# Loading and making in one program what the next one needs first: a chain of six on-chip programs

## The chip, the cores and the metric

One Trainium2 chip, one of its cores. The metric is the device time of one launch in microseconds. A core has five engines with instruction queues of their own: TensorE (PE: matrix products and transposes into PSUM banks), VectorE (DVE), ScalarE (ACT), GpSimd (POOL) and SyncE (SP), which issues the DMAs here. They are ordered against each other by semaphores alone.

## What is computed

A transformer-like chain over x of shape (16, 256, 128), with a context of (16, 64, 128). Every step is `x = x + f(layernorm(x))`:

```python
x = x + _L0_xattn_ref(_layernorm(x), ctx, mask, Wq, Wkv, Wout, b_out)      # cross attention, 16 heads
x = x + _L0_ffn_ref(_layernorm(x), Wqkv, q_scale, k_scale, Wo, ...)        # 6 layers: local attention + gated FFN
x = x + _L1_xattn_ref(_layernorm(x), ctx, ctx, projection)                 # kernel (random feature) attention
x = x + _L1_ffn_ref(_layernorm(x), clip_x, clip_down, w_gate, w_up, w_down) # FFN with rounded weights
x = x + _L2_xattn_ref(_layernorm(x), ctx, Wk1, ..., gamma, beta)           # causal + context attention, 3 norms
x = x + _L2_ffn_ref(_layernorm(x), W_fc, ln_w, ln_b, W_proj)               # FFN with ternary weights
x = x + _L3_xattn_ref(_layernorm(x), ctx, W, b)                            # context attention
x = x + _L3_ffn_ref(_layernorm(x), Ws, bs, W1, b1, W2, b2)                 # 8 experts, top-k of the tokens each
```

In the six layers q and k are normed per head, scaled by q_scale and k_scale, and rotated by fixed tables (cosine, sine, a position's scale). The ternary weights are `sign(W) * min(round(|W| / (mean(|W|) + 1e-6)), 1)`, a mean over the whole matrix.

## The kernel before

x stays in SBUF as x_all (128 partitions, 32 tiles of 128 tokens by 128 features). The work goes over it in 8 passes of 512 tokens (4 tiles); several stages split the passes into two groups of Q = 4. Six programs run one after the other, each in a block of its own: every engine gets a list of instructions in an order written out by hand, with waits on semaphores (`wait_ge`) between engines. At the end of a block all engines meet, SyncE clears the program's semaphores one by one (`clear`), and the next block begins. Names of tiles carry the program's letter:

- **x_**, `cross_attention`. The key and query weights, and the value and output weights, are multiplied together first (`fold`); then for each of 64 half tiles TensorE makes scores, VectorE lowers and weighs them, ScalarE takes exponentials, TensorE mixes. VectorE writes the normed sum into s_all.
- **f_**, `shifted_layers`. 6 layers times 8 passes, run as a hardware loop of 48 passes. At its start it loads the rotation tables' constants (L664 to L667), the first layer's weights and the first layer's Wv and Wo; TensorE folds these pair by pair (L805), ScalarE copies them (L1494) into w_vo; VectorE multiplies six layers' tables (rot_all, L1134), SyncE writes them to DRAM (rot_dram, L680) and reads the first layer's back (L636). VectorE clears k_t, vo_off and x_shifted among others (L1121 to L1129). Every engine then adds to the counters that the loop expects. In the loop SyncE issues the shifts of values and x, and the next layer's weights.
- **k_**, `kernel_attention_and_ffn`. Loads the context twice (ctx_t, and ctx_1 with a column of ones), the projection and the weights; x_all plus s_all is formed by VectorE and GpSimd; phi_k comes from ctx_t and proj, its products with ctx_1 (`values`, L1827) need it and GpSimd's constants. ScalarE copies them, then norms x (L2059).
- **a_**, `two_attentions`. Norms, causal attention, context attention and a two-layer FFN in phases, group by group. `take_stats` and `roots` on VectorE (12 short instructions a root), norms on ScalarE (L2648), `scale_and_shift` of each norm (two products or sums of 128x512) on GpSimd (L2481, L2483), `last_sum` on VectorE (L2572).
- **g_**, `ternary_ffn`. Loads W_fc and W_proj, measures the mean (VectorE, then a partition_all_reduce on GpSimd), makes ternary weights, takes the statistics of x; then per pass: turn, up, gelu, norm of h, down, add.
- **y_, e_**, `experts`. Loads for the context attention, then the experts' weights; statistics of x, attention, routing, then selection and the experts.

The order at the start of ternary_ffn on VectorE, as an example of how such a queue is written:

```python
            measure()
            roots(0)
            make_ternary()
            roots(1)
            for i in range(1, PASSES + 4):
                if i <= PASSES:
                    roots_of_h(i - 1)
                if 3 <= i <= PASSES + 2:
                    add(i - 3)
```

## Time and profile before

| | |
|---|---|
| three runs | 4461.14, 4453.69, 4463.28 us; median 4461.14 |
| profiled execution | 4456.33 us, its span 4454.5 us |
| PE busy | 3964.2 us (89%) |
| DVE busy | 3584.2 us (80%) |
| ACT busy | 2960.2 us (66%) |
| POOL busy | 2206.9 us (50%) |
| mean granted clock of TensorE | 0.931 |
| DMA | 251.24 MB, mean 56 GB/s |

The span runs from the first to the last instruction. Busy shares are averages over six programs with different limits. The granted clock is a share of TensorE's full speed; 0.5 would be the lower of its two levels all the time. In the rows further down, `PEld` is TensorE's weight load, `SPq` a DMA issued on SyncE's queue, `L830` a line of the kernel; `f_bank<-f_w_qk,f_xs_t` is output and inputs; `x2` the instructions in the row; in brackets stands the idle time of that engine just before, and what ended it.

### The profile page before, as it was taken

The numbers are of one execution on the slowest core, as the hardware profiler recorded it, in microseconds if no ns is written. First come the engines' busy times: TensorE is split into PE (matmuls) and PEld (weight loads), VectorE is DVE, ScalarE is ACT, GpSimd is POOL, SyncE is SP. The second block draws the span as 40 slices with busy tenths as digits, with TensorE's granted clock in tenths as the row PEclk, the third lists the DMA queues.
The fourth block names the chain that finished last, engine by engine and source line by source line (L and its number), as shares of the span: only waits on it lengthen the run. The fifth ranks groups of instructions, "written<-read, shape, count | busy, mean of one in ns | idle before, by whom it ended". The sixth has DMA issues, their size and how long they took to land. (4 is left out here: it accounts for less than half of the span.)

```text
span 4454.5 us, 117888 instructions
## 1 busy us (share of the span) xinstructions
PE 3964.2 (89%) x43247; PEld 2386.8 (54%) x43247; DVE 3584.2 (80%) x8496; ACT 2960.2 (66%) x5496; POOL 2206.9 (50%) x1392
## 2 busy tenths in 40 slices
PE   8978999999999999999999999999999855737735
PEld 5644555555555555555555555555555533525534
DVE  6887999899998999989999899989999655356341
ACT  3425787787777777777787787777778545636402
POOL 0005666666666666666666666666666400130006
PEclk9989999999999999999999999999999966868658
DMA  1012232333233332233232332232323200000102
GB/s 43 1 40 65 66 68 64 83 68 69 65 69 82 69 70 65 65 84 70 65 68 64 83 73 64 64 85 65 70 64 68 50 15 12 1 5 18 72 7 37
DMA packets 188120, 251.24 MB, mean 56 GB/s; under 512 B 88676, under 2 KB 129382, under 8 KB 187366
## 3 DMA queue, kind: packets, MB, share of 16 engines
q1 hardware_dynamic: 182054, 240.47, 23.2%
q0 software_dynamic: 5632, 4.33, 0.7%
q8 instruction: 352, 5.77, 0.6%
q14 instruction: 82, 0.67, 0.0%
HBM read 41.65 MB, written 14.30 MB: 13 GB/s over the span
## 5 line engine op out<-in xcount | busy, mean ns | idle before, releaser
L1419 POOL TENSOR_TENSOR f_rot_a<-f_rot_a,f_rot_b 128x1024 f32<-128x1024 f32 x384 | 908.1, 2370 | 311.8 <-DVE f_rot_b L1160 206.6
L1427 POOL TENSOR_TENSOR f_rot_a<-f_rot_a,f_norm 128x1024 f32<-128x1024 f32 x384 | 731.3, 1905 | 648.5 <-DVE f_norm L1178 525.4
L844 PE MATMUL f_bank<-f_w_vo,f_xs_t 128*32 128x512 f32 x6144 | 815.8, 603 | 0.2
L1157 DVE TENSOR_TENSOR f_rot_a<-f_bank,f_rot 128x512 f32<-128x512 f32 x768 | 523.0, 682 | 76.2 <-ACT f_squares L1519 40.4
L1528 ACT ACTIVATE f_vo<-f_bank 128x512 f32<-128x512 f32 x768 | 458.6, 597 | 170.2 <-PE f_bank L844 162.6
L1519 ACT ACTIVATE f_squares<-f_bank 128x512 f32<-128x512 f32 x768 | 455.8, 594 | 113.1 <-PE f_bank L830 67.1
L1540 ACT ACTIVATE f_k_t<-f_bank 64x512 f32<-64x512 f32 x768 | 452.7, 589 | 102.7 <-PE f_bank L866 98.2
L1160 DVE TENSOR_TENSOR f_rot_b<-f_bank,f_rot 128x512 f32<-128x512 f32 x768 | 505.9, 674 | 0.0
L1433 POOL TENSOR_TENSOR f_prob<-f_score,f_stat 128x512 f32<-128x512 f32 x384 | 400.6, 1043 | 192.1 <-DVE f_stat L1210 187.7
L1164 DVE TENSOR_REDUCE f_sums<-f_squares 128x16 f32<-128x1024 f32 x384 | 464.5, 1210 | 4.7 <-ACT f_squares L1519 4.7
L876 PEld LDWEIGHTS f_bank<-f_k_t,f_q_t 128*32 128x32 f32 x12288 | 345.4, 110 | 179.4 <-issue 99.5
L900 PEld LDWEIGHTS f_bank<-f_vo_off,f_prob_t 128*32 128x32 f32 x6144 | 330.8, 110 | 167.3 <-issue 150.7
L830 PE MATMUL f_bank<-f_w_qk,f_xs_t 128*128 128x512 f32 x768 | 400.5, 603 | 22.2 <-DMA f_w_qk<-in_Wqk 7.9
L876 PE MATMUL f_bank<-f_k_t,f_q_t 128*32 128x128 f32 x12288 | 406.0, 273 | 1.2 <-ACT f_bank L1546 0.6
L900 PE MATMUL f_bank<-f_vo_off,f_prob_t 128*32 128x128 f32 x6144 | 406.8, 274 | 0.2
L900 PE MATMUL f_bank<-f_vo,f_prob_t 128*32 128x128 f32 x6144 | 406.8, 274 | 0.0
L836 PE MATMUL f_bank<-f_w_qk,f_xs_t 128*128 128x512 f32 x768 | 401.7, 605 | 0.7 <-DVE f_rot_b L1160 0.7
L1533 ACT ACTIVATE f_q_t<-f_bank 128x512 f32<-128x512 f32 x384 | 227.9, 594 | 260.2 <-PE f_bank L860 260.2
L900 PEld LDWEIGHTS f_bank<-f_vo,f_prob_t 128*32 128x32 f32 x6144 | 330.8, 110 | 0.0
L1206 DVE TENSOR_REDUCE f_stat<-f_score 128x8 f32<-128x512 f32 x384 | 259.9, 677 | 76.8 <-ACT f_score L1550 71.9
L866 PEld LDWEIGHTS f_bank<-ident,f_rot_a 128*128 128x128 f32 x1536 | 180.4, 141 | 217.7 <-issue 153.8
L1198 DVE TENSOR_REDUCE f_stat<-f_bank 128x8 f32<-128x512 f32 x384 | 257.7, 671 | 29.1 <-PE f_bank L876 23.6
(446 smaller groups left out, 7372.8 us busy)
## 6 DMA issues: line engine op xcount, KB each, us to landing
f_vo_off<-f_vo SPq DMA_DIRECT2D x1152, 128.0 KB, 2.3
f_vo_off<-f_vo SPq DMA_DIRECT2D x384, 64.0 KB, 2.0
f_w_qk<-in_Wqk SPq DMA_DIRECT2D x12, 512.0 KB, 5.3
f_vo_dram<-f_vo_pair SPq DMA_DIRECT2D x48, 128.0 KB, 1.8
f_x_shifted<-s_all SPq DMA_DIRECT2D x48, 128.0 KB
f_x_shifted<-s_all SPq DMA_DIRECT2D x48, 127.0 KB
f_w_vo<-f_vo_dram SPq DMA_DIRECT2D x10, 512.0 KB, 5.4
e_w<-in_e_W SPq DMA_DIRECT2D x2, 2048.0 KB, 12.7
```

What stands on the lines that cost most here:

```text
L836: nc.tensor.matmul(flat(Q), chunk_x(t), w_qk[:, 0, 512 * g:512 * g + 512], start=True, stop=True).then_inc(q_done, 1)
L844: done = nc.tensor.matmul(bank[V][32 * w:32 * w + 32, :], x[:, at:at + 32], w_vo[:, 4 * g:4 * g + 4, w // 2, :], start=True, stop=True)
L876: done = nc.tensor.matmul(bank[S][32 * w:32 * w + 32, 128 * b:128 * b + 128], q_t[:, g, 128 * b + 32 * w:128 * b + 32 * w + 32], k_t[:, :, ...
L900: done = nc.tensor.matmul(bank[Y][32 * w:32 * w + 32, 0:128], prob_t[:, g, 128 * b + 32 * w:128 * b + 32 * w + 32], source[:, g, 2 * (t % ...
L1157: nc.vector.tensor_tensor(rot_a[:, slot, n, :].rearrange("p (h d) -> p h d", h=GROUP), source, c_tab, ALU.mult)
L1160: nc.vector.tensor_tensor(rot_b[:, g, n, :].rearrange("p (h s d) -> p h s d", h=GROUP, s=2), swapped, s_tab, ALU.mult).then_inc((q_rotated ...
L1164: nc.vector.tensor_reduce(sums[:, g, :], squares[:, g, :, :].rearrange("p n (h d) -> p (n h) d", h=GROUP), AX_X, ALU.add).then_inc(lengths, 1)
L1419: nc.gpsimd.tensor_tensor(rot_a[:, slot, :, :], rot_a[:, slot, :, :], rot_b[:, g, :, :], ALU.add).then_inc(rot_summed, 1)
L1427: nc.gpsimd.tensor_tensor(heads, heads, over(norm[:, 16 * g:16 * g + 16], [128, 16, HEAD_DIM]), ALU.mult).then_inc(qk_normed, 1)
L1519: nc.scalar.activation(squares[:, g, n, :], flat((Q, K)[n]), ACT.Square).then_inc((q_squared, k_squared)[n], 1)
L1528: nc.scalar.activation(vo[:, g, 2 * (t % 2) + j, :], flat(V), ACT.Copy).then_inc((va_copied, vb_copied)[j], 1)
L1540: done = nc.scalar.activation(k_t[r:r + 64, n, 4 * g:4 * g + 4, at:at + 128], flat(T)[r:r + 64, :].rearrange("p (b n) -> p b n", b=4), ACT ...
```

## The change

What a program needs first is loaded or made in the one ahead, in tiles that outlive it; the context (ctx_t, ctx_1) is held from the first program to the last.

- `cross_attention` gets, behind its x loads: the tables' constants, the first layer's Wv, Wo and other weights, ctx_1; GpSimd makes the mask `band` and the six tables one by one, SyncE writes them and reads the first back; TensorE folds the first layer's Wv and Wo behind its last mixing, ScalarE copies them.
- `shifted_layers` loses all of that. Its ScalarE shifts the first x before it adds to its counters. The clears of k_t, vo_off and x_shifted go from VectorE to GpSimd. SyncE issues four loads for kernel_attention_and_ffn ahead of the last layer.
- `kernel_attention_and_ffn` loses its loads and the waits for them.
- `two_attentions` loses the load of ctx_t, takes the first pass's root ahead of the others, loads the ternary program's weights and makes them ternary (in the tile h, which is not yet used), takes the next program's statistics, and in its second group gives the last scale and shift of every second pass to VectorE.
- `ternary_ffn` loses its loads, statistics and ternary weights; it loads for `experts` and takes the statistics and the first half of the roots for it.
- `experts` loses its six small loads, the statistics and the first roots.

The diff, cut to its core:

```diff
+            sp.wait_ge(fold_made, 4)
+            sp.dma_start(rot_const, dram["rot"]).then_inc(const_in, 16)
+            sp.dma_start(head_scale, dram["qk_scale"]).then_inc(const_in, 16)
+            sp.dma_start(band_in[:, :, :], dram["band"]).then_inc(const_in, 16)
+            sp.wait_ge(fold_made, 8)
+            sp.dma_start(w_v[:, :, :], dram["Wv_t"][0:PAIRS].rearrange("b p n -> p b n")).then_inc(next_in, 16)
+            for n in range(2):
+                half = slice(64 * n, 64 * n + 64)
+                sp.dma_start(w_out[half, :, n, :], dram["Wo"][0:PAIRS].rearrange("b p n -> p b n")[half]).then_inc(next_in, 16)
...
+            sp.dma_start(kept["w_qk"][:, :, :], first_of("Wqk").rearrange("a p n d -> (a p) n d")).then_inc(kept_in, 16)
...
+            for layer in range(DEPTH):
+                sp.wait_ge(rot_made, layer + 1)
+                sp.dma_start(rot_dram[layer], rot_part[layer % 2]).then_inc(rot_out[layer % 2], 16)
+            sp.wait_ge(rot_out[0], 16 * (DEPTH // 2))
+            sp.wait_ge(rot_out[1], 16 * (DEPTH // 2))
+            sp.dma_start(kept["rot"][:, :, :, :].rearrange("p a n d -> p (a n d)"), rot_dram[0]).then_inc(kept_in, 16)
+            sp.wait_ge(kept_in, 112)
...
+            pool.wait_ge(zeroed, 4)
+            pool.wait_ge(const_in, 48)
+            nc.gpsimd.tensor_copy(kept["band"][:, :, :], band_in[:, :, :]).then_inc(band_made, 1)
+            pool.wait_ge(band_made, 1)
+            for layer in range(DEPTH):
+                if layer > 0:
+                    pool.wait_ge(rot_made, layer)
+                if layer >= 2:
+                    pool.wait_ge(rot_out[layer % 2], 16 * (layer // 2))
+                nc.gpsimd.tensor_tensor(rot_part[layer % 2].rearrange("p (a n d) -> p a n d", a=2, n=4), rot_const,
+                                        head_scale[:, layer].unsqueeze(1).broadcast_to([128, 2, 4, 64]), ALU.mult).then_inc(rot_made, 1)
...
+            def fold_next(b):
+                if b == 0:
+                    pe.wait_ge(next_in, 48)
+                if b < 2:
+                    pe.wait_ge(unit_made, 8 * PASSES)
+                else:
+                    pe.wait_ge(lowered, N - 3 + b)
+                to = (unit_bank + score_bank)[b]
+                for k in range(2):
+                    last = nc.tensor.matmul(to[:, 256 * k:256 * k + 256], w_v[:, 2 * b + k, :], w_out[:, 2 * b + k, :, :], start=True, stop=True)
+                last.then_inc(next_folded, 1)
...
+            for b in range(4):
+                fold_next(b)
...
+                act.wait_ge(next_folded, b + 1)
+                nc.scalar.activation(w_vo_next[:, 2 * b:2 * b + 2, :, :].rearrange("p b n d -> p (b n d)"), (unit_bank + score_bank)[b][:, :], ACT.Copy).then_inc(next_made, 1)
...
             sp.wait_ge(zeroed, 2)
             load_pair(0)
-            sp.wait_ge(rot_made, DEPTH)
-            sp.dma_start(rot_dram.rearrange("l p n -> p l n"), rot_all.rearrange("p l a n d -> p l (a n d)")).then_inc(rot_out, 16)
-            sp.wait_ge(rot_out, 16)
-            load_rot(0, 0)
-            load_rot(1, 0)
-            for semaphore in (w_qk_in[0], w_qk_in[1], ln_in, w_2_in, rot_in[0], rot_in[1]):
-                good_for_layer(semaphore, 0)
-            good_for_layer(w_1_in, 0, 32)
+            for semaphore in (w_qk_in[0], w_qk_in[1], w_vo_in[0], w_vo_in[1], ln_in, w_2_in, rot_in[0], rot_in[1]):
+                sp.sem_inc(semaphore, PASSES * 16)
+            sp.sem_inc(w_1_in, PASSES * 32)
+            sp.wait_ge(off_zeroed, 2)
...
+            for name, to in following["loads"]:
+                sp.dma_start(to, dram[name]).then_inc(following_in, 16)
...
-            nc.vector.memset(wo_first, 0.0).then_inc(zeroed, 1)
-            chain.mark(nc.vector.memset(xs_t[:, :, :], 0.0))
+            nc.vector.memset(xs_t[:, :, :], 0.0).then_inc(zeroed, 1)
+            nc.vector.memset(wo_pair[:, :, :], 0.0).then_inc(zeroed, 1)
             chain.mark(nc.vector.memset(gate[:, :, :], 0.0))
-            chain.mark(nc.vector.memset(wo_pair[:, :, :], 0.0))
-            chain.mark(nc.vector.memset(k_t[:, :, :, :], 0.0))
-            chain.mark(nc.vector.memset(vo_off[:, :, :, :], 0.0))
-            chain.mark(nc.vector.memset(x_shifted[:, :, :], 0.0))
             chain.wait()
             chain.mark(nc.vector.memset(gate[ONES_ROW:ONES_ROW + 1, 2, :], 1.0))
-            dve.wait_ge(const_in, 48)
-            chain.link(nc.vector.tensor_copy(band[:, :, :], band_in))
-            nc.vector.nop().then_inc(zeroed, 1)
-            for layer in range(DEPTH):
-                nc.vector.tensor_tensor(rot_all[:, layer], rot_const, head_scale[:, layer].unsqueeze(1).broadcast_to([128, 2, 4, HEAD_DIM]), ALU.mult).then_inc(rot_made, 1)
-            dve.wait_ge(rot_made, DEPTH)
...
+            pool.wait_ge(x_taken[0], 1)
+            nc.gpsimd.memset(k_t[:, :, :, :], 0.0).then_inc(k_t_cleared, 1)
+            pool.wait_ge(k_t_cleared, 1)
+            nc.gpsimd.memset(vo_off[:, :, :, :], 0.0).then_inc(off_zeroed, 1)
+            pool.wait_ge(off_zeroed, 1)
+            nc.gpsimd.memset(x_shifted[:, :, :], 0.0).then_inc(off_zeroed, 1)
+            pool.wait_ge(off_zeroed, 2)
...
-            for b in range(4):
-                act.wait_ge(first_folded, b + 1)
-                nc.scalar.activation(w_vo[:, 2 * b:2 * b + 2, :, :].rearrange("p b n d -> p (b n d)"), flat(b), ACT.Copy).then_inc(w_vo_in[b // 2], PASSES * 8)
             act.wait_ge(zeroed, 2)
             act.wait_ge(s_opened, 1)
-            act.wait_ge(rot_out, 16)
+            def shift_in(s, p):
+                act.wait_ge(x_turned[s], p + 1)
+                source = bank[F][:, 0:SEQ]
+                nc.scalar.activation(xs_t[0:64, s, :], source[0:64, :], ACT.Copy).then_inc(xs_made[s], 1)
+                nc.scalar.activation(xs_t[64:128, s, 1:SEQ], source[64:128, 0:SEQ - 1], ACT.Copy).then_inc(xs_made[s], 1)
+            shift_in(0, 0)
...
+            sp.dma_start(next_w[:, 0, :], dram["g_fc"]).then_inc(next_in, 16)
+            sp.dma_start(next_w[:, 1, :], dram["g_proj"]).then_inc(next_in, 16)
+            sp.dma_start(following["affine"][:, :, :], dram["g_affine"]).then_inc(next_in, 16)
...
-                for i in range(Q):
+                for i in range(0, Q, 1 if g == 0 else 2):
...
+            def next_stats(p, count):
+                dve.wait_ge(summed, count)
+                at = PASS_TILES * (p % Q)
+                for t in range(PASS_TILES):
+                    chain.mark(nc.vector.bn_stats(stats[:, 0, at + t, :], tile(of_pass(x_all, p), t)))
+                chain.wait()
+                for t in range(PASS_TILES):
+                    chain.mark(nc.vector.bn_aggr(following["mv"][:, PASS_TILES * p + t, :], stats[:, 0, at + t, :]))
+            def measure():
+                dve.wait_ge(next_in, 48)
+                nc.vector.tensor_reduce(size[:, :, 0], next_w, AX_X, ALU.add, apply_absolute_value=True).then_inc(sized, 1)
+            def make_ternary():
+                dve.wait_ge(size_sum, 1)
+                chain.link(nc.vector.tensor_scalar(size[:, :, 2], size[:, :, 1], 1.0 / (DIM * PASS_TOK), 1e-6, ALU.mult, ALU.add))
+                chain.link(nc.vector.reciprocal(size[:, :, 3], size[:, :, 2]))
+                for k in range(2):
+                    chain.mark(nc.vector.tensor_scalar(w_tern[:, k, :], next_w[:, k, :], size[:, k, 3:4], 0.5, ALU.mult, ALU.is_gt))
+                chain.wait()
+                for k in range(2):
+                    chain.mark(nc.vector.tensor_scalar(next_w[:, k, :], next_w[:, k, :], size[:, k, 3:4], -0.5, ALU.mult, ALU.is_lt))
+                chain.wait()
+                nc.vector.tensor_tensor(w_tern[:, :, :], w_tern[:, :, :], next_w, ALU.subtract).then_inc(tern_made, 1)
+            def scale_and_shift(p):
+                dve.wait_ge(hatted[3], p + 1)
+                tiles = [128, PASS_TILES, 128]
+                source, to = (ap.rearrange("p (t n) -> p t n", n=128) for ap in (hat[:, p % Q, :], n[:, p % Q, :]))
+                chain.wait()
+                dve.wait_ge(y3_made, p + 1)
+                chain.link(nc.vector.tensor_tensor(to, source, rows[:, GAMMA, :].unsqueeze(1).broadcast_to(tiles), ALU.mult))
+                chain.link(nc.vector.tensor_tensor(to, to, rows[:, BETA, :].unsqueeze(1).broadcast_to(tiles), ALU.add))
...
             def phase_0(g):
                 for i in range(Q):
                     take_stats(0, Q * g + i, of_pass(x_all, Q * g + i))
-                roots(0, g, 1e-5)
+                    if g == 0 and i == 0:
+                        roots(0, g, 1e-5, slice(0, PASS_TILES))
+                roots(0, g, 1e-5, slice(0 if g else PASS_TILES, GROUP_TILES))
...
             def phase_6(g):
-                for i in range(Q):
-                    last_sum(Q * g + i)
+                if g == 0:
+                    for i in range(Q):
+                        last_sum(i)
+                    for i in range(Q):
+                        next_stats(i, Q)
+                else:
+                    for p in range(Q, PASSES, 2):
+                        scale_and_shift(p + 1)
+                        last_sum(p + 1)
+                        next_stats(p + 1, p + 1)
+                        last_sum(p)
+                        next_stats(p, p + 2)
             phase_0(0)
-            dve.wait_ge(first_in, 112)
+            dve.wait_ge(first_in, 96)
             nc.vector.tensor_copy(causal[:, :], causal_in[:, :]).then_inc(causal_made, 1)
             phase_0(1)
+            measure()
             dve.wait_ge(rest_in, 80)
             nc.vector.tensor_tensor(beta_b2[:, :], rows[:, BETA, :], rows[:, B2, :], ALU.add).then_inc(beta_made, 1)
             for i in STEPS:
                 phase_2(0, i)
+            make_ternary()
...
-            measure()
             roots(0)
-            make_ternary()
             roots(1)
             for i in range(1, PASSES + 4):
                 if i <= PASSES:
                     roots_of_h(i - 1)
                 if 3 <= i <= PASSES + 2:
                     add(i - 3)
+                    next_stats(i - 3)
+                    if i - 3 == Q:
+                        next_roots()
         @block.scalar
...
-            for g in range(GROUPS):
-                for p in range(Q * g, Q * g + Q):
-                    take_stats(Y, p)
-                roots(Y, g)
+            roots(Y, 1)
...
+                    by, on = shift[:, k, at:at + 1], var[:, k, 1, at:at + 1]
+                    if k == Y and p < Q:
+                        by, on = given["shift"][:, at:at + 1], given["var"][:, 1, at:at + 1]
...
```

## Rows read from the trace of the kernel before

**Rows 1.** Windows by stage: us, busy us per engine, granted clock, DMA share, GB/s.
```profile
344.70:3586.80 3242.10, 3189.05 (x39070) 1844.09 (x39068) 2916.44 (x6208) 2471.75 (x4508) 2048.03 (x1247) 0.99 0.30 68
```

**Rows 2.** Timeline, end of the first program, start of the layers program.
```profile
304.96 2.05 PE L296 MATMUL x_bank<-x_vo,x_prob_t 128*128 128x128 f32 x16
...
310.09 1.12 DVE L375 TENSOR_SCALAR s_all<-x_all,x_s_mv,x_s_var 128x128 f32<-128x128 f32 x4
313.65 0.33 SPq L664 DMA_DIRECT2D f_q_t<-in_rot  x1
...
319.25 3.90 DVE L1125 MEMSET f_k_t<- 128x4608 f32 x1 [0.91 <-issue]
...
339.45 0.81 SPq L636 DMA_DIRECT2D f_rot<-f_rot_dram  x2
...
341.91 2.04 PE L830 MATMUL f_bank<-f_w_qk,f_xs_t 128*128 128x512 f32 x2 [7.46 <-ACT f_xs_t L1510]
...
348.31 2.36 POOL L1419 TENSOR_TENSOR f_rot_a<-f_rot_a,f_rot_b 128x1024 f32<-128x1024 f32 x1 [13.85 <-DVE f_rot_b L1160]
```

**Rows 3.** Timeline, first 60 us: a fold on TensorE, a GpSimd memset.
```profile
10.05 0.94 POOL L204 MEMSET x_w_q<- 64x1024 f32 x1
...
27.96 3.62 PE L235 MATMUL x_bank<-x_w_out,x_w_v 128*128 128x256 f32 x16
```

**Rows 4.** Timeline, start of the kernel-attention program.
```profile
3598.44 0.20 POOL L1813 MEMSET k_ones<- 128x128 f32 x1
...
3604.46 7.06 PE L1827 MATMUL k_bank<-k_ctx,k_phi_k 64*32 64x129 f32 x32 [0.77 <-ACT k_phi_k L2140]
```

**Rows 5.** Timeline, start of the two-attentions program.
```profile
3758.49 6.26 ACT L2648 ACTIVATE a_xn<-x_all,a_shift,a_var 128x128 f32<-128x128 f32 x16 [13.24 <-DVE a_shift L2514]
```

**Rows 6.** Timeline of VectorE, middle of the two-attentions program.
```profile
3826.01 0.42 DVE L2536 TENSOR_REDUCE a_top<-a_bank 128x4 f32<-128x256 f32 x1 [9.71 <-PE a_bank L2354]
```

**Rows 7.** Timeline of VectorE, its second half begins.
```profile
3916.46 0.68 DVE L2528 TENSOR_TENSOR a_y<-a_att,a_xn 128x512 f32<-128x512 f32 x1
...
3922.17 0.39 DVE L2536 TENSOR_REDUCE a_top<-a_bank 128x4 f32<-128x256 f32 x1
```

**Rows 8.** Timeline of all engines, end of the two-attentions program.
```profile
3986.56 1.26 POOL L2481 TENSOR_TENSOR a_n<-a_hat,a_rows 128x512 f32<-128x512 f32 x1
3986.63 1.74 DVE L2572 SCALAR_TENSOR_TENSOR x_all<-a_n,x_all 128x512 f32<-128x512 f32 x1 [4.48 <-POOL a_n L2483]
...
3995.30 0.69 DVE L2572 SCALAR_TENSOR_TENSOR x_all<-a_n,x_all 128x512 f32<-128x512 f32 x1 [1.15 <-POOL a_n L2483]
```

**Rows 9.** Timeline, start of the ternary program.
```profile
3999.33 0.33 SPq L2860 DMA_DIRECT2D g_w<-in_g_fc  x1
...
4004.12 0.86 DVE L2923 BATCH_NORM_STATS2 g_stats<-x_all 128x6 f32<-128x128 f32 x4
...
4008.95 0.17 DVE L2934 TENSOR_SCALAR g_var<-g_mv 128x16 f32<-128x16 f32 x1
...
4011.52 3.19 ACT L2994 ACTIVATE g_xn<-x_all,g_shift,g_var 128x128 f32<-128x128 f32 x8 [22.99 <-DVE g_shift L2936]
...
4013.57 1.23 DVE L2949 TENSOR_TENSOR g_w_tern<-g_w_tern,g_w_cmp 128x1024 f32<-128x1024 f32 x1
...
4016.00 0.60 ACT L3001 ACTIVATE g_xn_t<-g_bank 128x512 f32<-128x512 f32 x1 [1.29 <-PE g_bank L2875]
```

**Rows 10.** Timeline of VectorE, end of ternary, start of the last.
```profile
4090.24 2.47 DVE L2955 BATCH_NORM_STATS2 g_h_stats<-g_h 128x6 f32<-128x512 f32 x4 [2.87 <-ACT g_h L3008]
...
4109.35 0.69 DVE L2974 TENSOR_TENSOR x_all<-x_all,g_bank 128x512 f32<-128x512 f32 x1 [6.71 <-PE g_bank L2890]
```

**Rows 11.** Timeline of ScalarE, start of the last program.
```profile
4120.76 1.65 ACT L3303 ACTIVATE y_xn<-x_all,y_shift,y_var 128x128 f32<-128x128 f32 x4 [15.34 <-DMA y_ctx_rows<-in_ctx_rows]
```

**Rows 12.** Timeline of SyncE, start of the last program.
```profile
4111.52 0.33 SPq L3127 DMA_DIRECT2D y_w<-in_y_W  x1
```

**Rows 13.** One line of VectorE in the layers program.
```profile
L1171 DVE TENSOR_SCALAR f_norm_y<-f_norm_y x194: 170/181/2324, 353.7 to 3557.2; 128x32 int32<-128x32 int32 x146, 128x36 int32<-128x36 int32 x46, 128x4 int32<-128x4 int32 x2
```

255 lines of the change are left out of this document (111 added, 144 removed).

## The prediction

> **What bounds the kernel now.** I read the windows by stage first. The layers program takes 3242 us with TensorE busy for 3189 of them at a granted clock of 0.99 [rows 1]; the loads and first steps of every program lie outside that stretch, so its steady loop gets nothing from this change and no edit is aimed at it. What is left is the seams between the six programs, and there I read the timeline of all engines. At the first seam VectorE ends the first program at 311.2, SyncE issues the first load of the next at 313.65, but TensorE starts projecting only at 341.91, because ScalarE waits for a round trip of the rotation tables through DRAM, whose last leg is issued at 339.45 [rows 2]. In the other seams the reader is to see who holds the first norm or product: in kernel-attention the product of phi_k and the context's values, at 3604.46 [rows 4]; in the ternary program VectorE's statistics and roots, ScalarE's norm following at 4011.52 and its copy of the turned tile at 4016.00 [rows 9]; in the last program a DMA, to 4120.76 [rows 11].
>
> **The change part by part, and its sum.** Times are of the profiled execution.
>
> *First program's end.* Behind the last mixing product (ends 307.0 [rows 2]) TensorE gets four folds of two products each, the 16 matmuls that take 3.62 us in [rows 3]; ScalarE's last copy then ends near 307.0 + 3.6 + 0.8 = 311.4 to 311.5, against VectorE's 311.2 [rows 2]: +0.3. At the lower clock the folds could take twice that: bound +3.9. The loads for it (SyncE issues twelve for constants, weights and context, six writes of tables and one read back) come after the x loads; nothing stands behind them on SyncE but the end of the program, 260 us later. GpSimd's cast and six products lie in the first 60 us or so; each can hold a VectorE operation of two SBUF inputs as the 1.74 against 0.69 in [rows 8] shows, 1.05 us for at most seven: 0 to +7, and I take +0.5, since most of VectorE's work there reads PSUM or one input. Semaphores are cleared one by one: 3.34 us lie between VectorE's end at 3995.99 [rows 8] and the next program's 3999.33 [rows 9], 52 semaphores, and 1.48 between 4110.04 [rows 10] and 4111.52 [rows 12], 18 semaphores: 0.055 each. Nine more here: +0.5.
>
> *Start of the layers.* Gone are the wait for first_in, eight folds, six table products and the round trip. What still stands before the first projection, from SyncE's 313.65: VectorE starts 0.5 later and clears xs_t, wo_pair and gate (0.48, 0.27, 1.34, 0.17 of gap, 0.48 by size, at the 0.85 ns an element of the 3.90 us clear [rows 2]), then adds to its counters; SyncE's three loads and counters and ScalarE's two copies end sooner. So TensorE begins near 313.65 + 3.7 = 317.4 instead of 341.91: -24.5. GpSimd now clears k_t, vo_off and x_shifted, 9216 elements a partition at 0.94 us for 1024 [rows 3], 8.5 us behind its 0.4 us copy: free near 323.2. Its first sum was at 348.31 [rows 2], so it is due at 323.8: covered by 0.6 us. Were that cover gone and the clears to count in full: +8. What waits for them on other queues (ScalarE's first k copy, SyncE's first shift) comes later still.
>
> *In the layers.* Four loads for kernel-attention are issued on SyncE ahead of the last layer, some 0.4 us each; behind them stand the shifts of values. SyncE waits for ScalarE there, so 0, with +1.7 as the bound.
>
> *Kernel-attention.* Its products of phi_k no longer wait for the context's load. Next to be late is GpSimd's last constant, done at 3598.64, against 3604.46 [rows 4]: -5.7. ScalarE's chain of copies, norms and rounding follows on it; the roots it needs next do not depend on a load and were done before the products began to matter.
>
> *Two attentions, start.* The roots are split, one pass first. VectorE's second root chain costs another 2.45 us (that of 16 tiles, 4008.95 to 4011.4 [rows 9]), so the norms of passes 1 to 3 start at 3758.5 + 2.45 = 3760.9. Three passes of 6.26 / 4 us [rows 5] end at 3765.6, against 3764.7: ScalarE's copy of the turned tile stands behind all four norms, so the early start of one buys nothing: +0.9.
>
> *Two attentions, middle.* The ternary weights take about 3.5 us of VectorE (4011.3 to 4014.8, [rows 9]), behind the second phase; VectorE has 9.7 us of idle time before 3826.01 [rows 6]: 0. The statistics of the first four passes (4004.12 to 4008.95, 4.8 us, [rows 9]) stand ahead of VectorE's additions from 3916.46, and it goes from these without a gap into the scores at 3922.17, for which ScalarE and TensorE wait [rows 7]: +4.8, in full.
>
> *Two attentions, end.* GpSimd's four passes of two 1.26 us products become two, VectorE takes the other two and all statistics: the roots end at 3982.15 (3986.63 less the 4.48 of idle time), ScalarE's second norm 3.1 us later, and from there on, 3985.4, it has four products (0.69), four sums (0.69) and four times 1.2, 10.3 us, ending at 3995.7, as before [rows 8] if nothing collides. But a VectorE operation with two SBUF inputs, begun under a GpSimd product, ended 0.55 us behind it (1.74 instead of 0.69, [rows 8]). Followed through, three such meetings add 1.0 us each: ends 0 to +5, taken +3.0. This is what the Trainium skill, SBUF — State Buffer, section Who interferes with whom, says: the two engines exclude each other for the whole instruction when VectorE has two SBUF inputs. It speaks against giving VectorE this work; by it the term is +3, without it 0.
>
> *Ternary program.* Only the roots stay before the first norm: 3999.4 + 2.5 = 4001.9, two norms of 3.19 us to 4005.1, then the copy that came at 4016.00 [rows 9]: -10.9. Statistics for the next program (1.2 a pass) fit the idle time before the next statistics of h, 2.87 us at the shortest [rows 10]; where next_roots (2.45) is added they do not: 1.2 + 2.45 - 2.87 = +0.8. The last pass has no cover, +1.2.
>
> *Last program.* ScalarE's first norm at 4111.6 instead of 4120.76 [rows 11, 12]: -9.1; the expert weights' loads move ahead and are needed much later. Five semaphores fewer over the later programs: -0.3.
>
> Sum: 0.3 + 0.5 + 0.5 - 24.5 - 5.7 + 0.9 + 4.8 + 3.0 - 10.9 + 0.8 + 1.2 - 9.1 - 0.3 = -38.5. The profiled execution took 4456.3 (4454.5 of span and 1.8 around it): 4417.8. It lies 4.8 below the median of three runs, 4461.1; from that, 4422.6. I take 4420.
>
> **Rivals.**
> 1. GpSimd becomes the bound at the start of the layers: its clears cost more than 9 us and the counters that wait for them hold the first shift. For it: the cover is only 0.6 us. Against it: the price is read from like clears. +8: 4428.
> 2. The change does less than it says: a program's first instructions come late for reasons other than its data. In the layers' start TensorE waited for ScalarE, but ScalarE's own 6 us were for nothing the trace names, and some of it may be its long row of counters, which still stands there. A third of -24.5 lost, and part of the others: +12, 4432.
> 3. Slower. The layers' 48 passes of 67.5 us [rows 1] are entered with GpSimd and VectorE at another phase to each other. VectorE's L1171 usually takes 0.18 us but once 2.32, under a GpSimd sum [rows 13]; if the loop locks into such meetings, +0.8 us a pass undoes all, and +0.9 gives 4420 + 43 = 4463. Against it: the loop is TensorE's, busy for 98% of it, and its order is unchanged.
> 4. No change within the measurement: the same at +0.8 a pass.
>
> **How the numbers follow.** Forecast 0.70, rival 1 0.12, rival 2 0.10, rival 3 0.05, rival 4 0.03. Below the forecast lie the case without collisions (-3), and the runs' own spread (4453.7 to 4463.3); so 4404 at the low end. Upward the bounds of the folds, of GpSimd's work in the first program and rivals 1 and 2: 4440. About 0.2% (9 us) is what a measurement of this kernel can tell from no change: faster 0.92, same 0.03, slower 0.05.
>
> **What would show it.** The layers' first projection some 4 us after the program's first instruction; in kernel-attention the phi_k products right behind GpSimd's last constant; in two attentions the four norms ending about 1 us later, 4.8 us of statistics ahead of the second half's additions, the last sums of x_all at VectorE and not GpSimd; the ternary program's first copy under 7 us from its start; the last program's first norm at once. The layers' stretch of about 3242 us must stand. It is wrong if that moves by over 10 us, if the first seam keeps more than 10 us, or if GpSimd's or VectorE's operations grow in the first program.

## The result, and the profile after

The changed kernel takes 4416.48 us (median of four runs, 4414.45 to 4419.71) where the kernel before took 4461.64 (four runs, 4453.69 to 4463.28): 45.2 us less, a ratio of 0.990 with a 95% interval from 0.9888 to 0.9912. The profiled execution took 4414.45, its span 4412.6, against 4456.33 and 4454.5: 41.9 less. Two further sets of runs of the changed kernel gave 4415.14 and 4415.52, against 4463.02 and 4461.80 of the kernel before beside them. The 4463.02 is the median of the seven fast runs of that control, without two slow ones of 5139.95 and 12955.43 us.

To see where the time went I read the same event in both timelines, one seam after the other, and note how much earlier it comes in the kernel after. All rows until the experiments are of the profiled execution of the kernel after, in its timeline, unless said otherwise.

**Something nobody edited comes first.** Before (first fence), GpSimd stands idle for 7.67 us ahead of the select that makes the identity matrix, and every engine's first program waits for that; after (second fence), it stands idle for 0.51 us. The first load is issued at 2.60 instead of 9.77: 7.17 us, and the prediction has no word of it.

```profile
8.76 0.28 POOL L3697 TENSOR_SCALAR_AFFINE_SELECT ident<-ident 128x128 f32<-128x128 f32 x1 [7.67 <-issue]
```

```profile
1.59 0.29 POOL L3746 TENSOR_SCALAR_AFFINE_SELECT ident<-ident 128x128 f32<-128x128 f32 x1 [0.51 <-POOL ident_bf L3743]
...
2.60 0.39 SPq L195 DMA_DIRECT2D x_w_k<-in_x_Wk  x1
```

**The first seam** (answers to [rows 2] and [rows 3]). The folds are there, 3.62 us, and the last copy of them ends at 305.62, under VectorE's last operation, 305.72: they cost nothing. VectorE's first operation of the layers comes at 309.46, TensorE projects at 312.14, where it was at 341.91. GpSimd's clears end at 318.10; behind them it copies x once more, until 318.66, which the prediction's account leaves out, and its first sum follows on that without idle time, at 318.63. The rotation that the sum needs is done at 318.45. So nothing is left of the cover of 0.6 us that the prediction gave the clears.

```profile
299.47 2.05 PE L345 MATMUL x_bank<-x_vo,x_prob_t 128*128 128x128 f32 x16
...
301.36 3.62 PE L358 MATMUL x_bank<-x_w_out,x_w_v 128*128 128x256 f32 x16
...
304.61 1.11 DVE L439 TENSOR_SCALAR s_all<-x_all,x_s_mv,x_s_var 128x128 f32<-128x128 f32 x4
305.02 0.60 ACT L536 ACTIVATE f_w_vo<-x_bank 128x512 f32<-128x512 f32 x1 [0.27 <-PE x_bank L358]
...
309.46 0.48 DVE L1151 MEMSET f_xs_t<- 128x512 f32 x1 [3.74 <-PEq L66]
...
310.01 3.94 POOL L1434 MEMSET f_k_t<- 128x4608 f32 x1
...
312.14 2.04 PE L860 MATMUL f_bank<-f_w_qk,f_xs_t 128*128 128x512 f32 x2 [1.45 <-DVEq L1157]
...
317.17 1.28 DVE L1180 TENSOR_TENSOR f_rot_b<-f_bank,f_rot 128x512 f32<-128x512 f32 x2
...
318.27 0.39 POOL L1430 COPY f_xw<-s_all 128x256 f32<-128x256 f32 x1 [0.17 <-POOL f_x_shifted L1438]
...
318.63 2.35 POOL L1446 TENSOR_TENSOR f_rot_a<-f_rot_a,f_rot_b 128x1024 f32<-128x1024 f32 x1
```

In the first program itself one operation of VectorE shows GpSimd's new work, a product that takes 0.69 us elsewhere and began under a GpSimd product:

```profile
43.37 1.38 DVE L428 TENSOR_TENSOR x_prob<-x_score,x_stat 128x512 f32<-128x512 f32 x1
```

**The layers**, in the view by windows (answers to [rows 1]; from the first rotation to the last sum): 3242.07 us, TensorE busy for 3190.90, granted clock 0.99. The same two events lie 3241.34 apart before. The second row is a stretch of two attentions to which I come below.

```profile
314.96:3557.03 3242.07, 3190.90 (x39070) 1845.84 (x39068) 2916.83 (x6208) 2471.63 (x4508) 2051.65 (x1250) 0.99 0.30 68
3835.04:3866.43 31.39, 18.97 (x84) 13.21 (x83) 12.43 (x54) 14.77 (x34) 10.12 (x8) 0.73 0.00 1
```

**Kernel-attention** (answers to [rows 4]). The products of phi_k begin 0.05 us after GpSimd's last constant is done (3568.84 and 0.20). From the first row to the last, the first norm, 19.36 us pass; before it was 25.67 (3586.06 to 3611.73).

```profile
3557.03 0.69 DVE L1274 TENSOR_TENSOR s_all<-s_all,f_bank 128x512 f32<-128x512 f32 x1 [4.76 <-PE f_bank L981]
3561.98 0.10 POOL L1820 MEMSET k_plus<- 128x1 f32 x1 [56.33 <-POOLq L66]
...
3568.84 0.20 POOL L1825 MEMSET k_ones<- 128x128 f32 x1
...
3569.09 7.08 PE L1839 MATMUL k_bank<-ctx,k_phi_k 64*32 64x129 f32 x32 [3.48 <-POOL k_ones L1825]
...
3576.39 3.17 ACT L2069 ACTIVATE k_xn<-x_all,k_shift,k_var 128x128 f32<-128x128 f32 x8
```

**Two attentions.** At its start (answers to [rows 5]) the first norm is early, the other three wait for the second root chain, and the copy of the turned tile is at 3729.26, 14.33 us after VectorE's first statistics; before it was 13.51.

```profile
3718.63 1.65 ACT L2716 ACTIVATE a_xn<-x_all,a_shift,a_var 128x128 f32<-128x128 f32 x4 [9.62 <-DVE a_shift L2529]
...
3724.63 4.72 ACT L2716 ACTIVATE a_xn<-x_all,a_shift,a_var 128x128 f32<-128x128 f32 x12 [4.35 <-DVE a_shift L2529]
...
3729.26 0.57 ACT L2733 ACTIVATE a_xn_t<-a_bank 128x512 f32<-128x512 f32 x1
```

In the middle (answers to [rows 7]) 4.7 us of statistics (L2597) stand between the last sum of x_all and the additions, and the scores at 3893.21 come after them all:

```profile
3882.08 0.69 DVE L2590 SCALAR_TENSOR_TENSOR x_all<-a_n,x_all 128x512 f32<-128x512 f32 x1 [1.17 <-POOL a_n L2496]
3882.81 0.87 DVE L2597 BATCH_NORM_STATS2 a_stats<-x_all 128x6 f32<-128x128 f32 x4
...
3887.52 0.66 DVE L2543 TENSOR_TENSOR a_y<-a_att,a_xn 128x512 f32<-128x512 f32 x1
...
3893.21 0.39 DVE L2551 TENSOR_REDUCE a_top<-a_bank 128x4 f32<-128x256 f32 x1
```

At the end (answers to [rows 8]) VectorE's products and GpSimd's hold each other: VectorE's take 1.66 and 1.70 us where 0.69 is the usual price, and its next sum 1.63. The program ends 19.54 us after its last roots begin (3950.67 to 3970.21); before it was 16.31 (3979.68 to 3995.99).

```profile
3956.32 1.26 POOL L2496 TENSOR_TENSOR a_n<-a_n,a_rows 128x512 f32<-128x512 f32 x1
3956.48 1.66 DVE L2625 TENSOR_TENSOR a_n<-a_hat,a_rows 128x512 f32<-128x512 f32 x1 [3.33 <-ACT a_hat L2716]
3958.06 1.26 POOL L2494 TENSOR_TENSOR a_n<-a_hat,a_rows 128x512 f32<-128x512 f32 x1 [0.47 <-ACT a_hat L2716]
3958.17 1.70 DVE L2626 TENSOR_TENSOR a_n<-a_n,a_rows 128x512 f32<-128x512 f32 x1
...
3969.83 0.38 DVE L2600 BATCH_NORM_AGGREGATE g_mv<-a_stats 128x2 f32<-128x6 f32 x4
```

**Ternary and last program** (answer to [rows 9] and [rows 10 to 12]). Only roots stand ahead of the first norm; the copy comes 5.65 us after the program's first instruction at 3973.77, where it took 16.67. The last pass's statistics are uncovered, and then the last program norms at once.

```profile
3973.82 0.17 DVE L3003 TENSOR_SCALAR g_var<-g_mv 128x16 f32<-128x16 f32 x1 [3.61 <-PEq L66]
...
3976.33 3.18 ACT L3051 ACTIVATE g_xn<-x_all,g_shift,g_var 128x128 f32<-128x128 f32 x8 [16.81 <-DVE g_shift L3005]
...
3979.42 0.57 ACT L3058 ACTIVATE g_xn_t<-g_bank 128x512 f32<-128x512 f32 x1
```

```profile
4073.49 0.69 DVE L3030 TENSOR_TENSOR x_all<-x_all,g_bank 128x512 f32<-128x512 f32 x1 [5.39 <-PE g_bank L2952]
4074.22 0.87 DVE L2986 BATCH_NORM_STATS2 g_next_x_stats<-x_all 128x6 f32<-128x128 f32 x4
...
4076.85 1.65 ACT L3353 ACTIVATE y_xn<-x_all,yg_shift,yg_var 128x128 f32<-128x128 f32 x4 [7.28 <-PEq L66]
```

This table puts all traces of this study side by side, those of the experiments too. Each column is the distance between two events, in us: the start until the first load's issue; x from there to the last s_all operation of the first program; "to rot" from there to the layers' first rotation; the layers to their last sum; k to the last sum of kernel-attention; the gap to the first statistics of two attentions; a to the first norm of the ternary program; g to the first norm of the last one; y to the memset of ec_ones; and the rest of the span.

| trace | start | x | to rot | layers | k | gap | a | g | y | rest | span |
|---|---|---|---|---|---|---|---|---|---|---|---|
| before | 9.77 | 300.32 | 34.63 | 3241.34 | 161.47 | 3.62 | 260.37 | 109.24 | 130.90 | 202.84 | 4454.5 |
| before, again | 9.86 | 300.89 | 34.63 | 3241.54 | 161.82 | 3.62 | 261.23 | 107.76 | 131.70 | 205.55 | 4458.6 |
| before, no sum over partitions | 2.61 | 300.87 | 34.59 | 3247.66 | 162.03 | 3.63 | 261.33 | 107.36 | 133.86 | 203.66 | 4457.6 |
| first seam only | 9.80 | 303.58 | 10.28 | 3243.06 | 160.39 | 4.17 | 263.46 | 106.83 | 133.91 | 203.32 | 4438.8 |
| all but the first seam | 2.60 | 300.76 | 34.29 | 3244.52 | 154.77 | 3.52 | 264.32 | 100.59 | 132.26 | 203.87 | 4441.5 |
| after | 2.60 | 302.01 | 10.35 | 3242.07 | 154.25 | 3.65 | 261.40 | 100.52 | 132.35 | 203.40 | 4412.6 |
| after, again | 2.60 | 301.43 | 10.35 | 3241.88 | 154.26 | 3.65 | 261.41 | 100.52 | 132.37 | 203.23 | 4411.7 |
| after, third | 2.60 | 302.07 | 10.35 | 3244.15 | 154.82 | 3.64 | 259.73 | 99.35 | 132.17 | 205.42 | 4414.3 |
| clear of k_t twice | 2.60 | 302.88 | 10.35 | 3241.39 | 154.38 | 3.64 | 264.50 | 100.60 | 132.34 | 203.82 | 4416.5 |
| spare sum over partitions | 9.16 | 301.86 | 10.35 | 3244.14 | 154.14 | 3.65 | 259.77 | 99.36 | 133.76 | 204.51 | 4420.7 |
| statistics late | 2.61 | 300.89 | 10.35 | 3240.46 | 154.12 | 3.64 | 256.27 | 99.41 | 132.20 | 205.65 | 4405.6 |
| three pieces put otherwise | 2.60 | 301.99 | 10.35 | 3246.64 | 154.85 | 3.65 | 256.37 | 99.21 | 133.73 | 204.81 | 4414.2 |
| the same, again | 2.60 | 302.62 | 10.35 | 3238.03 | 154.80 | 3.64 | 256.36 | 99.20 | 133.69 | 204.21 | 4405.5 |

Between the rows "before" and "after" lie -7.2, +1.7, -24.3, +0.7, -7.2, 0.0, +1.0, -8.7, +1.4 and +0.6: -41.9 in all.

### The profile page after: what moved, and what is told of

Same layout as the page of the kernel before. It is cut to its first block and busy times, and to the rows that moved or that the text cites. A ratio compares the mean times of both kernels' runs of the same rounds, so it can differ in the third digit from the quotient of the medians.

```text
span 4412.6 us, 117906 instructions
## 1 busy us (share of the span) xinstructions
PE 3968.6 (90%) x43247; PEld 2389.2 (54%) x43247; DVE 3577.9 (81%) x8501; ACT 2960.0 (67%) x5496; POOL 2218.5 (50%) x1398
```

## The experiments

**The kernel before once more.** No edit; it is the control for the idle time at the start.

> The kernel before, once more, for its trace. The trace of before holds 7.67 us of idle time of GpSimd ahead of its first affine_select (line 3697), that of after 0.51 us there, though neither kernel was changed at that place. Theory A (it comes and goes between executions of any kernel): this trace may show either, and the other runs of this call a mixture. Theory B (it belongs to a program): about 7.7 us again here. Under B, 7.2 us of the 41.9 between the two profiled executions are not the seams' work but are still the changed program's; under A they are chance.

Measured: 4460.39 us (one run), and 7.76 us of idle time at that place. Against theory A, though one trace doesn't decide.

**The first seam alone.** The kernel before with the first program and the layers of the changed one; nothing is loaded in the layers for kernel-attention, and the context is loaded anew where it was.

```diff
-            cross_attention(nc, x_all, ident, arrays, s_all)
-            shifted_layers(nc, s_all, ident, ident_bf, arrays)
+            cross_attention(nc, x_all, ident, arrays, s_all, kept)
+            shifted_layers(nc, s_all, ident, ident_bf, arrays, kept, None)
```

> The kernel before with only the first part of the change: constants, rotation tables, folds and weights of the layers are made and loaded in the first program. Theory (each seam gives its own share): of the 41.9 us between the profiled executions 29.0 are there when the layers end, 7.2 of them at the very start; so 4461 - 22 = 4439 if the start is as in before, and 4432 if it is short, with the first projection under 4 us behind the layers' first instruction and the layers' stretch within 1.5 us of 3242. Rival (the layers lock into another phase against GpSimd): the stretch is over 10 us longer and the time over 4445.

Measured: 4442.60 us (five runs, 4436.50 to 4444.65) against 4459.98, ratio 0.9959 (0.9945 to 0.9972): 17.4 less. "To rot" is 10.28 as in the changed kernel, the layers' stretch 3243.06, the start long. So the seam gives what it should in its place and rival and theory part there in the theory's favour; but 5 us are lost elsewhere: x took 303.58, 2.9 more than the 300.7 on average of the four traces that have it unchanged, and two attentions, whose code is that of before, 263.46 instead of 260.4 to 261.3. The trace accounts for most of the 2.9: three of VectorE's products in the first program, 0.69 us alone, take 1.54, 1.28 and 1.75 under GpSimd's new operations, 2.5 us more.

**All but the first seam.** The changed kernel with the old first program (it loads the context's rows in addition) and the old start of the layers.

```diff
-                cross_attention(nc, x_all, ident, arrays, s_all, kept)
-                shifted_layers(nc, s_all, ident, ident_bf, arrays, kept, for_kq)
+            cross_attention(nc, x_all, ident, arrays, s_all, held)   # as before, and the rows of the context
+            shifted_layers(nc, s_all, ident, ident_bf, arrays, for_kq)   # as before, and the four loads ahead of the last layer
```

> The changed kernel with the first part undone: first program and start of the layers as before, all later seams as changed. Theory: the remaining 12.9 us of the trace, 4461 - 13 = 4448, and if the start is the short one 4441. Rival (the later seams give only part, some of it being clock): 4452 or more. With the first part alone the two gains should add up to the 45 us of the whole change within 5 us.

Measured: 4442.83 us (five runs, 4441.41 to 4444.06), ratio 0.9961 (0.9947 to 0.9974): 17.2 less, with the short start, where 4441 was expected; so the rival (4452 or more) falls. The two parts add up to 34.6, not to 45 within 5: additivity failed. The table says where. In the traces the two parts together are 28.7 and the whole 41.9; of the 13.2 between, 6.0 lie in two attentions (+3.1 and +4.0 in the parts, +1.0 in the whole), 4.2 in the layers (+1.7, +3.2, +0.7), 2.9 in y, 2.0 in x, less 2.3 in g, and the rest is small. None of that is at a seam: "to rot", k up to the first norm, and the ternary program's start are each what they are in the whole. This is a reading of one execution of each. But the medians of five runs are 10.6 us short as well, and the five of this kernel lie within 2.7 us, so the luck of one execution isn't enough to explain it. Why the parts give less than the whole isn't shown.

**Three pieces of two attentions put otherwise.**

```diff
 def phase_6(g):                       # g == 0
-                    for i in range(Q):
-                        next_stats(i, Q)
...
             roots(2, 1, EPS)
+            for i in range(Q):
+                next_stats(i, Q)
...
-                for i in range(0, Q, 1 if g == 0 else 2):      # GpSimd, last norm
+                for i in range(Q):
...
-                        scale_and_shift(p + 1)                 # VectorE, last phase
-                        last_sum(p + 1)
-                        next_stats(p + 1, p + 1)
                         last_sum(p)
-                        next_stats(p, p + 2)
+                        next_stats(p, p + 1)
...
-                    if g == 0 and i == 0:
-                        roots(0, g, 1e-5, slice(0, PASS_TILES))
-                roots(0, g, 1e-5, slice(0 if g else PASS_TILES, GROUP_TILES))
+                roots(0, g, 1e-5)
```

> The changed kernel with three of its pieces in two attentions put otherwise: the statistics of the first four passes stand behind the roots of the second norm of the second half (8.90 us of idle VectorE there) instead of ahead of its additions; the last norm's scale and shift is GpSimd's alone again, VectorE keeping the sums and statistics; and the first roots are one chain. Theory: -4.9 (statistics hidden), -1.9 (the end of the program 17.6 us behind the last roots instead of 19.5), -0.8 (the first copy): 7.6 us less than the changed kernel, about 4409. Rival 1: the idle time is not free, since ScalarE or TensorE run ahead of what they did and meet VectorE elsewhere: half of it, 4412. Rival 2: the statistics between the sums delay GpSimd's chain at the end by 1.2 us a pass: nothing won there, 4411.

Measured: 4405.97 us (four runs, 4404.34 to 4416.04), ratio 0.9878 (0.9862 to 0.9893), where 4409 was expected and the rivals had 4411 and 4412. Each piece can be read where it stands (the code numbers the norms of two attentions from 0 to 3, and so do I). The roots of norm 3 in the first half and of norm 1 in the second lie 32.14 us apart instead of 36.98: -4.84. The timeline of VectorE shows the statistics in their new place, done 4.2 us before anything is due:

```profile
3928.24 0.18 DVE L2529 SCALAR_TENSOR_TENSOR a_shift<-a_mv,a_var 128x16 f32<-128x16 f32 x1
3928.33 0.86 DVE L2594 BATCH_NORM_STATS2 a_stats<-x_all 128x6 f32<-128x128 f32 x4
...
3932.74 0.38 DVE L2597 BATCH_NORM_AGGREGATE g_mv<-a_stats 128x2 f32<-128x6 f32 x4
3937.30 0.69 DVE L2575 SCALAR_TENSOR_TENSOR a_h<-a_h 128x512 f32<-128x512 f32 x1 [4.19 <-ACT a_h L2803]
```

The end comes 17.69 us behind the last roots (3952.65 to 3970.34) instead of 19.54: -1.85. Here VectorE's statistics (0.87 for four, as without company) run under a GpSimd product undisturbed, while its sum, which reads two tiles, takes 1.65:

```profile
3960.87 1.59 POOL L2496 TENSOR_TENSOR a_n<-a_n,a_rows 128x512 f32<-128x512 f32 x1
3961.37 0.87 DVE L2594 BATCH_NORM_STATS2 a_stats<-x_all 128x6 f32<-128x128 f32 x4
...
3962.42 1.25 POOL L2494 TENSOR_TENSOR a_n<-a_hat,a_rows 128x512 f32<-128x512 f32 x1
3962.57 1.65 DVE L2587 SCALAR_TENSOR_TENSOR x_all<-a_n,x_all 128x512 f32<-128x512 f32 x1
...
3969.96 0.38 DVE L2597 BATCH_NORM_AGGREGATE g_mv<-a_stats 128x2 f32<-128x6 f32 x4
```

And the first copy comes 13.50 us after the first statistics instead of 14.33: -0.83. The sum of the three is 7.5, against 7.6 expected, so both rivals fall. The profiled execution was at the same time the slowest of the four (its layers took 3246.64).

**GpSimd's clear of k_t twice.**

```diff
+            nc.gpsimd.memset(k_t[:, :, :, :], 0.0).then_inc(off_zeroed, 1)
+            pool.wait_ge(off_zeroed, 1)
             nc.gpsimd.memset(k_t[:, :, :, :], 0.0).then_inc(k_t_cleared, 1)
...   # the later waits for off_zeroed go up by one
```

> The changed kernel with GpSimd's clear of k_t, 3.94 us, done twice at the start of the layers. In the changed kernel GpSimd was free at 318.66 and its first sum began at 318.63, so the cover is gone already. Theory (GpSimd's clears are now on the path there): the first sum comes 13.3 us behind the layers' first instruction instead of 9.3, and the end of the first pass, 217.3 us behind it, comes 3 to 4 us later. Rival (the wait is taken up by TensorE's row of passes, since the first sum feeds only a later product): the first sum is late and the first pass ends less than 1 us later.

Measured: 4418.30 us (one run). GpSimd's clears and its first two sums:

```profile
310.88 3.94 POOL L1434 MEMSET f_k_t<- 128x4608 f32 x1
...
314.88 3.94 POOL L1436 MEMSET f_k_t<- 128x4608 f32 x1
...
318.88 3.51 POOL L1438 MEMSET f_vo_off<- 128x4096 f32 x1
...
323.49 4.66 POOL L1448 TENSOR_TENSOR f_rot_a<-f_rot_a,f_rot_b 128x1024 f32<-128x1024 f32 x2
```

The first sum is 13.3 us behind TensorE's first instruction (310.20), as the theory says, and yet the first pass ends 216.99 us behind it (527.19), against 217.33 in the changed kernel (309.33 to 526.66). The theory falls and the rival stands: 4 us of delay on GpSimd at the start of the layers cost nothing. GpSimd's own idle stretches take them up. In the changed kernel it waits 2.61 us for VectorE ahead of its second sum and 7.77 us ahead of a later product:

```profile
323.60 2.34 POOL L1446 TENSOR_TENSOR f_rot_a<-f_rot_a,f_rot_b 128x1024 f32<-128x1024 f32 x1 [2.61 <-DVE f_rot_b L1180]
...
343.66 1.90 POOL L1454 TENSOR_TENSOR f_rot_a<-f_rot_a,f_norm 128x1024 f32<-128x1024 f32 x1 [7.77 <-DVE f_norm L1198]
```

With the second clear the two sums run back to back (x2 above), so the second is late by 1.3 us only, counted from TensorE's first instruction, and the product at the second place comes 0.4 us early, behind 6.11 us of idle time.

**The sum over partitions: left out before, doubled after.** Two kernels.

```diff
 # the kernel before, ternary program
-            nc.gpsimd.partition_all_reduce(size[:, :, 1], size[:, :, 0], 128, ...).then_inc(size_sum, 1)
+            nc.gpsimd.tensor_copy(size[:, :, 1], size[:, :, 0]).then_inc(size_sum, 1)
 # the changed kernel, ternary program
+            nc.gpsimd.memset(spare[:, :, 0], 1.0).then_inc(spare_set, 1)
+            pool.wait_ge(spare_set, 1)
+            nc.gpsimd.partition_all_reduce(spare[:, :, 1], spare[:, :, 0], 128, ...).then_inc(spare_set, 1)
```

> The kernel before, in which the ternary program's sum over partitions on GpSimd is left out (a plain copy stands in its place, so the weights' mean size is a partition's own). The idle time ahead of the first affine_select was 7.67, 7.76 and 7.71 us in the three traces in which that sum stands in the ternary program, and 0.51, 0.51 and 0.50 in the three in which it stands in two attentions, two programs of other loads. Theory A (the sum over partitions, by its place, makes GpSimd wait at the start): 0.5 us here. Theory B (something else in the text of the later programs, as how GpSimd's instructions lie): 7.7 us again.

> The changed kernel with a second sum over partitions on GpSimd, of a spare tile, in the ternary program, where the kernel before has its own. Theory A (that place makes the start slow): 7.7 us of idle time ahead of the first affine_select. Theory B (the place doesn't matter, only the first one or the order of the instructions does): 0.5 us as in the changed kernel. Either way the ternary program's start should not move by over 1 us.

Measured: the kernel before without the sum, 4459.39 us (one run), has the short start (first fence); the changed kernel with a spare sum in the ternary program, 4422.54 (one run), has a long one (second fence). Theory A holds both times, though the wait brought back is 7.06 us and not the 7.7 expected.

```profile
1.60 0.29 POOL L3697 TENSOR_SCALAR_AFFINE_SELECT ident<-ident 128x128 f32<-128x128 f32 x1 [0.51 <-POOL ident_bf L3694]
```

```profile
8.15 0.28 POOL L3754 TENSOR_SCALAR_AFFINE_SELECT ident<-ident 128x128 f32<-128x128 f32 x1 [7.06 <-issue]
```

Over all thirteen traces the start is long, 7.06 to 7.76 us of idle time, in the four whose ternary program has a sum over partitions, and 0.50 or 0.51 in the nine where it has none; the sum in two attentions, one program earlier, brings no such wait. The total doesn't always show it: without the sum the kernel before saved 7.2 at the start and had the longest layers of all, 3247.66.

**The changed kernel twice more, and the pieces on one chip.** The first has no edit, nor has the second; the third has only the first piece of the three, the fourth is the kernel with three pieces again. The last three ran on one chip.

> The changed kernel once more, for a second trace and for its time on the chip on which these run. Theory: the short start (0.5 us ahead of the first affine_select) again, 4416 within 4 us, 44 to 46 below the kernel before; the layers' 47 intervals between ends of passes add up to 3030 to 3034 us, the difference all at the five changes of layer. Rival (part of the 45 was this chip's or these runs' luck): a ratio nearer to 1 than 0.992.

> The changed kernel a third time, on the same chip as the next two, to compare these with it. Theory: 44 to 46 us below the kernel before. Two attentions, from its first statistics to its last, took 254.9 us in both traces of the changed kernel so far (3714.93 to 3969.83 and 3714.17 to 3969.08) but 258.0 with the second clear, at a place that the clear doesn't touch; so 254.9 to 258.0 here.

> The changed kernel with one piece moved: the statistics of the first four passes for the ternary program stand behind the roots of the second norm of the second half, in 8.90 us of idle VectorE, instead of ahead of the additions of the second half. Theory (they stand on the path where the change put them): 32.1 us instead of 37.0 between the first roots of the third norm and the roots of the first norm of the second half, as in the run with three pieces put otherwise, and about 4.9 us less than the changed kernel on this chip. Rival (they fill a wait there that comes back elsewhere): under 2 us less.

> The kernel with three pieces put otherwise once more, on the same chip as the changed kernel. Theory: 7.5 us less than the changed kernel (4.84, 1.85 and 0.83 us, each read in its place in the first trace of it); the first comparison, over two chips, gave 9 to 10. Rival (part of what the first comparison showed was the chip's): 4 to 5 us less only. It should beat both kernels, the one before by 50 to 54 us.

Measured:

| kernel | us, median (runs) | from, to | ratio to before, 95% |
|---|---|---|---|
| after, again | 4415.14 (5) | 4413.50, 4419.80 | 0.9900, 0.9885 to 0.9915 |
| after, third | 4415.52 (4) | 4414.24, 4421.48 | 0.9901, 0.9884 to 0.9917 |
| statistics late | 4414.05 (4) | 4407.43, 4416.12 | 0.9896, 0.9880 to 0.9913 |
| three pieces, again | 4408.01 (4) | 4407.14, 4411.06 | 0.9883, 0.9867 to 0.9900 |

The short start comes again, and the gain with it, 47.9 and 46.3 us against the runs of before beside them, a little above the 44 to 46 expected; the rival of luck falls. The layers' intervals add up to 3030.25 us, as expected. The three pieces give 7.5 us on one chip, the sum read in place, and all their runs there lie below all those of the changed kernel: it is the version that beats both, 53.8 us below the kernel before. The late statistics alone are undecided by the time: 1.5 us by the medians, which is what the rival has (under 2), but in a row of runs 9 us wide. In the trace the stretch between the two roots, of norm 3 and norm 1, is 32.17 us against 35.87 and 36.98 in the traces of the changed kernel, so the piece does give 3.7 to 4.8 at its place, and a column of 256.3 in a where the changed kernel has 259.7 to 261.4. The bound of 254.9 to 258.0 for two attentions was missed from below: 253.24 (3717.63 to 3970.87).

## Why the prediction was right, and where only by balance

It said 4420 with the range 4404 to 4440, and the sum for the profiled execution 4417.8; measured were 4416.48 and 4414.45. Point by point, each with the distance in the two traces that answers to it:

| step | predicted | measured |
|---|---|---|
| folds at the first program's end | +0.3 | 0.0 |
| GpSimd's work in the first program | +0.5 | +1.7 (x); +1.4 over nine traces with it and four without |
| nine more semaphores, VectorE's gap | +0.5 | +0.8 (2.95 to 3.74) |
| start of the layers, from the last s_all to the first rotation, gap included | -24.0 | -24.3 |
| loads ahead of the last layer | 0 | not to be seen |
| kernel-attention up to its first norm | -5.7 | -6.3, of it -0.6 in the gap before |
| two attentions, start | +0.9 | +0.8 |
| ternary weights in its middle | 0 | 0.0 (77.39 to 77.37 us between the roots around them) |
| statistics of the first half's passes | +4.8 | +4.8 (32.15 to 36.98); +3.7 in the third trace (35.87) |
| its end | +3.0 | +3.2 (16.31 to 19.54) |
| ternary program, start | -10.9 | -11.0 (16.67 to 5.65) |
| next_roots and statistics in its passes | +0.8 | +0.7 (93.35 to 94.07) |
| last pass's statistics | +1.2 | +1.2 (2.17 to 3.33) |
| last program's norm | -9.1 | -9.2 (9.24 to 0.03) |
| five semaphores fewer over the later programs | -0.3 | +0.2 in the gap before the ternary program (3.34 to 3.56; two attentions has four more); the other gaps are in the rows above |

The row of the first rotation holds that of the nine semaphores, so that one isn't added again. The terms sum to -38.5 as predicted and to about -38.4 as measured (1.7 - 24.3 - 6.3 + 0.8 + 4.8 + 3.2 - 11.0 + 0.7 + 1.2 - 9.2; the gap before the ternary program adds 0.2, so -38.2). The mechanism was right at every seam, and no term of one is off by more than 0.7. The largest miss among the terms is "GpSimd's work in the first program", +0.5 taken and +1.7 found in x; but only 0.7 of it is GpSimd's, in one meeting with VectorE (1.38 instead of 0.69). That is still the growth of a VectorE operation in the first program which the prediction named as a sign of being wrong; its cost stayed within the 0 to 7 us given there. In the nine traces with this work one to three products of this line are held, nearly all to between 0.98 and 1.75 us, and in the four without it none. Together they add 0.7 to 2.5 us to a trace, 1.3 on average, of the +1.4 in the table: over many executions this is where the term was too small. Another 1.3 us of this trace come before GpSimd has any new work, so they aren't its (0.3 is won back later): TensorE's first product comes 0.35 later behind the first load's issue, and the four copies of its folds (L481) are 1.70, 1.71 and 1.28 us apart, where they were 1.70, 1.22 and 0.86. What slows TensorE there I can't say. The first product comes 6.8 to 8.2 us behind the first load's issue over the thirteen traces, with the old and the new program mixed, so the 0.35 is within what the same code does.

What the prediction lacked altogether is two things of opposite sign. The move of the ternary weights took the sum over partitions out of the ternary program, and with it 7.2 us at the very start; the experiments show that this is the cause, not why a late sum makes the first select wait. And the stretches that the prediction left at their old time aren't constant: +0.7 in the layers, +1.6 in the first half of two attentions, +1.4 and +0.6 in the last program, less 0.9 in kernel-attention: +3.4. -38.2 - 7.2 + 3.4 = -42.0, and 41.9 were read. So the step that failed is the assumption, made without a word, that all between the seams keeps its time; its two parts, -7.2 and +3.4, half cancel, and the 4420, already set between 4417.8 and 4422.6 for the spread of the runs, came out 3.5 high. That is luck: in the medians the gain is 45.2 where the sum has 38.5, and those 6.7 us are close to the 7.2 of the start, which comes in every trace of the changed kernel, while the +3.4 belongs to these two executions.

Of the rivals, the first (GpSimd's clears become the bound) was rightly feared in its place, the cover being gone at 318.63, and wrongly priced: it took a delay there to count in full, and a further 4 us cost nothing. The second (the change does less) fell: "to rot" gives all of the 24. The third (slower, a locked phase in the layers) fell: within a layer, from its third pass on, the ends of passes lie 65.85 to 65.88 us apart in every trace, before and after. The 67.5 us a pass that it reckoned with are 3242 over 48, with the ramp and the changes of layer in them. The fourth (no change) falls with the time. The +3.2 at the end of two attentions came about by the meetings that were foreseen, and the rule weighed there was that of the Trainium skill, SBUF — State Buffer, section Who interferes with whom. By that rule VectorE is held where it reads two tiles of SBUF; this trace agrees, with 1.63 to 1.70 us for operations that take 0.69 alone (1.74 in [rows 8]). In the trace of the three pieces the statistics, which read one tile, keep their 0.87 for four. But reading one tile doesn't spare every operation: at the start of the layers VectorE's L1191, usually 0.18 us, takes 2.32 under GpSimd's second sum (323.60 to 325.94) and ends with it, as L1171 did in [rows 13].

```profile
323.66 2.32 DVE L1191 TENSOR_SCALAR f_norm_y<-f_norm_y 128x32 int32<-128x32 int32 x1
```

What the prediction didn't draw from the rule is that the split of the last norm then costs more than it brings: GpSimd alone is 1.85 us faster.

## What to carry to other kernels

Work moved ahead of a seam is paid where it lands: all of the 24 us at the first seam came, because the new place had TensorE and ScalarE free under VectorE's tail, while 8 us of the later seams' gain were given back, 4.8 of them because statistics were put on the path some 44 us ahead of 8.9 us of idle time. Before placing such work, list the idle stretches of its engine in the program ahead and take the one behind the data, not the nearest. And when the trace after disagrees in a place that nobody edited, look there first: here 7.2 us at the very start were the larger part of the surprise.
